# Larger weight-quantisation pieces, a direct attention evacuation, and DMA transposes for three quarters of the gate and up weights

## The reference

```python
scores = einsum(q, k) * 64**-0.5 * exp(-alpha * |i - j|)      # 16 heads of 64
x = layernorm(x + softmax(scores) @ v @ Wo.T + bo)
g = silu(fp4(x) @ fp4(w_gate).T);  u = fp4(x) @ fp4(w_up).T   # w_gate, w_up: 2816 x 1024
x = layernorm(x + fp4(g * u) @ fp4(w_down).T)                 # w_down: 1024 x 2816
```

## Time and profile before

| what | value |
|---|---|
| median of 2 runs | 3286.92 us (3286.06 to 3287.78) |
| the profiled execution, time | 3282.99 us |
| its span, slowest core (core 4) | 3281.4 us |
| spans of the other cores | 3273.2 to 3279.9 us |
| PE busy | 1607.8 us (49%), 7186 instructions |
| DVE busy | 2270.2 us (69%), 3480 instructions |
| ACT busy | 985.7 us (30%), 924 instructions |
| mean granted PE clock | 0.68 of full |

### The profile page before, as it was taken

One profiled execution on the slowest core, in us unless ns is written; L12 is line 12 of the kernel. 1 busy time (PEld: TensorE's weight loads), 2 busy tenths in 40 slices (PEclk: granted clock), 3 DMA queues, 4 the chain that ended last, 5 costly groups with the idle time before them and its releaser, 6 DMA issues.

```text
span 3281.4 us, 26766 instructions; the slowest of 8 cores (3273.2 to 3281.4 us)
## 1 busy us (share of the span) xinstructions
PE 1607.8 (49%) x7186; PEld 548.2 (17%) x7186; DVE 2270.2 (69%) x3480; ACT 985.7 (30%) x924; POOL 36.1 (1%) x61
## 2 busy tenths in 40 slices
PE   5776555555555555555540010000036666663298
PEld 2331111111111111111210000000012222221143
DVE  2006777778777877777358878888868888888223
ACT  1223444444444444444241111111112222222022
POOL 0000000000000000000000000000000000000000
PEclk9886555665566666565775555555568888887599
DMA  5110000000000000000441111111100111111344
GB/s 77 26 26 21 17 19 18 17 19 18 17 19 18 18 19 20 20 20 13 107 153 38 39 52 38 39 39 39 39 13 19 39 38 47 37 39 38 114 172 159
DMA packets 93220, 141.24 MB, mean 43 GB/s; under 512 B 59922, under 2 KB 59922, under 8 KB 93074
## 3 DMA queue, kind: packets, MB, share of 16 engines
q1 hardware_dynamic: 77442, 90.76, 9.0%
q0 software_dynamic: 11024, 31.99, 4.1%
q10 hardware_dynamic: 4608, 16.78, 1.3%
HBM read 104.35 MB, written 36.18 MB: 43 GB/s over the span
## 4 chain that ended last, share of the span: by engine, by line
DVE 53%; PE 19%; issue 14%; ACT 7%; DMA 6%; DVEq 2%; SPq 1%; ACTq 0%; POOL 0%; POOLq 0%
DVE SDr L525 15%; PE ps_o L929 5%; DVE qc L188 4%; DVE qxn L158 4%; DVE qr L151 4%; PE ps_q L328 3%; ACT PT L537 3%; DVE qc L178 2%; DVE qm L183 2%; DVE qc L185 2%; DVE qc L160 2%; PE ps_tp L216 2%; PE ps_av L473 2%; PE ps_q L348 2%; DVE qm L173 2%
## 5 line engine op out<-in xcount | busy, mean ns | idle before, releaser
L525 DVE TENSOR_TENSOR SDr<-ps_s,Wd 128x512 f32<-128x512 f32 x1024 | 637.1, 683 | 251.9 <-PE ps_s L499 218.7
L537 ACT ACTIVATE PT<-SDr 128x2048 bf16<-128x2048 f32 x256 | 474.8, 1902 | 331.2 <-DVE SDr L525 331.2
L499 PE MATMUL ps_s<-QT,KT 64*128 64x512 bf16 x1024 | 280.9, 540 | 453.6 <-DVE SDr L525 452.2
L473 PE MATMUL ps_av<-PT,VV 128*64 128x512 bf16 x1024 | 294.0, 566 | 149.2 <-ACT recD L559 149.2
L164 ACT ACTIVATE qcc<-qc 128x1024 bf16<-128x1024 bf16 (+1 forms) x84 | 99.0, 1179 | 887.8 <-DVE qc L160 887.8
L823 PE MATMUL ps_g<-wgT,x1qT 128*128 128x512 bf16 (+1 forms) x768 | 216.1, 436 | 178.6 <-DVE hbuf L842 178.0
L480 PE MATMUL ps_d<-PT,ones 128*64 128x512 bf16 x1024 | 290.7, 559 | 0.0
L216 PE MATMUL ps_tp<-idn,wqo 128*128 128x128 bf16 x352 | 51.9, 291 | 462.8 <-DVE wqo L189 433.9
L499 PEld LDWEIGHTS ps_s<-QT,KT 64*128 64x128 bf16 x1024 | 59.3, 99 | 815.1 <-issue 815.0
L829 PE MATMUL ps_u<-wuT,x1qT 128*128 128x512 bf16 (+1 forms) x768 | 185.7, 389 | 0.0
L929 PE MATMUL ps_o<-wdT,hin 128*128 128x512 bf16 x704 | 154.8, 384 | 3.2 <-DMA x1in<-x_scr 3.2
(11 more groups left out here) (111 smaller groups left out, 2212.1 us busy)
## 6 DMA issues: line engine op xcount, KB each, us to landing
wst<-wu SPq DMA_DIRECT2D x11, 1024.0 KB
hqT_scr<-hqT POOLq DMA_DIRECT2D x16, 704.0 KB, 3.4
hin<-hqT_scr SPq DMA_DIRECT2D x16, 704.0 KB
awst<-wd SPq DMA_DIRECT2D x16, 512.0 KB
xres<-x SPq DMA_DIRECT2D x16, 512.0 KB, 4.3
x_scr<-ra ACTq DMA_DIRECT2D x16, 512.0 KB, 2.8
x1sl<-x_scr SPq DMA_DIRECT2D x8, 1024.0 KB
x1in<-x_scr SPq DMA_DIRECT2D x16, 512.0 KB
```

The source lines that it names most:

```text
L473: p.do("tensor", lambda e, kt=kt, PT=PT, rq0=rq0, h=h: e.matmul(out=ps_av.ap()[rq0:rq0 + 64, :], lhsT=VVa[:, kt, h * 64:(h + 1) * 64], rhs ...
L499: e.matmul(out=ps.ap()[:, b2 * 512:b2 * 512 + QC], lhsT=KTa[rq0:rq0 + 64, hp, kt * 128:(kt + 1) * 128], rhs=QTa[rq0:rq0 + 64, hp, qc * QC: ...
L525: return e.tensor_tensor(out=SDr.ap()[:, s8 * 512:(s8 + 1) * 512], in0=ps.ap()[:, b2 * 512:b2 * 512 + QC], in1=wd_ap, op=ALU.mult)
L537: e.activation(out=PT.ap()[:, 4 * g * QC:(4 * g + 4) * QC], in_=SDr.ap()[:, r8 * 2048:(r8 + 1) * 2048], func=AF.Exp), sA, 1)
```

## The change

In the attention stage the quantisation scratch is widened from 1024 to 1408 columns, and `w_down` is cut into two pieces of 1408 a row tile, so there are 16 pieces for `w_down` where there were 24, and 24 in all where there were 32; their spacing is 21 steps. `avst` and its copy go: the last multiply of a unit reads `ps_av` in PSUM and waits for `recD`, ACT no longer waits for the earlier multiply, and PE's next accumulation into `ps_av` waits for the multiply (`evac_done`). In the gate and up weights 6 of the 8 column groups of each chunk are transposed by 12 DMAs on SP, and 2 groups remain with PE and DVE.

```diff
--- before.py
+++ after.py
@@ -384,16 +384,15 @@
                 p.wait("tensor", sA, sA_proj)
                 aq_es = ExitStack()
                 aq_sb = lambda n, sh, dt: aq_es.enter_context(nc.sbuf_tensor(n, sh, dt))
-                awst = aq_sb("awst", [128, 1024], F32)
-                awq = aq_sb("awq", [128, 1024], BF16)
-                aqxn = aq_sb("aqxn", [128, 1024], F32)
-                aqc1 = aq_sb("aqc1", [128, 1024], BF16)
-                aqc2 = aq_sb("aqc2", [128, 1024], BF16)
-                aqcc = aq_sb("aqcc", [128, 1024], BF16)
-                aqm = aq_sb("aqm", [128, 1024], I8)
-                aqr = aq_sb("aqr", [128, 64], F32)
-                aqs = aq_sb("aqs", [128, 64], F32)
-                avst = aq_sb("avst", [128, 512], F32)
+                awst = aq_sb("awst", [128, 1408], F32)
+                awq = aq_sb("awq", [128, 1408], BF16)
+                aqxn = aq_sb("aqxn", [128, 1408], F32)
+                aqc1 = aq_sb("aqc1", [128, 1408], BF16)
+                aqc2 = aq_sb("aqc2", [128, 1408], BF16)
+                aqcc = aq_sb("aqcc", [128, 1408], BF16)
+                aqm = aq_sb("aqm", [128, 1408], I8)
+                aqr = aq_sb("aqr", [128, 88], F32)
+                aqs = aq_sb("aqs", [128, 88], F32)
 
                 aqb = {"r": aqr.ap(), "s": aqs.ap(), "xn": aqxn.ap(),
                        "c1": aqc1.ap(), "c2": aqc2.ap(), "cc": aqcc.ap(),
@@ -404,9 +403,10 @@
                 wgq_r2 = wgq_dram.rearrange("(r p) c -> p r c", p=128)
                 aw_chunks = []
                 for rt in range(8):
-                    for (c0, ln) in ((0, 1024), (1024, 768), (1792, 1024)):
-                        aw_chunks.append((wd_r2[:, rt, c0:c0 + ln],
-                                          wdq_r2[:, rt, c0:c0 + ln], ln))
+                    for hf in range(2):
+                        aw_chunks.append((wd_r2[:, rt, hf * 1408:(hf + 1) * 1408],
+                                          wdq_r2[:, rt, hf * 1408:(hf + 1) * 1408],
+                                          1408))
                 for row in range(8):
                     aw_chunks.append((wg_r2[:, row, :], wgq_r2[:, row, :], 1024))
                 aw_load = {}
@@ -453,7 +453,7 @@
 
                 for k in range(len(aw_chunks)):
                     acts = aw_actions(k)
-                    base = k * 16
+                    base = k * 21
                     for oi, off in enumerate((0, 2, 4, 6, 8, 10, 12, 13)):
                         aw_sched[base + off] = acts[oi]
                 wd_stride = 3968
@@ -461,7 +461,6 @@
                 sd_kt = {0: 0, 1: 0, 2: 0}
                 exp_ring = {0: 0, 1: 0}
                 exps_grp = {}
-                evac1_done = {}
                 evac_done = {}
                 recd_done = {}
                 first_sd = True
@@ -507,7 +506,7 @@
                                 up = u - 1
                                 p.wait("tensor", sA, exps_grp[(up, kt // 4)])
                                 if kt == 0:
-                                    p.wait("tensor", sV, evac1_done.get(up - 1, 0))
+                                    p.wait("tensor", sV, evac_done.get(up - 1, 0))
                                     p.wait("tensor", sA, recd_done.get(up - 1, 0))
                                 emit_av_kt(up, kt)
                             p.wait("vector", sT, sT.n)
@@ -548,27 +547,21 @@
                         hp_, qc_ = units[up]
                         if u == len(units):
                             p.wait("tensor", sA, exps_grp[(up, 3)])
-                            p.wait("tensor", sV, evac1_done.get(up - 1, 0))
+                            p.wait("tensor", sV, evac_done.get(up - 1, 0))
                             p.wait("tensor", sA, recd_done.get(up - 1, 0))
                             for kt in range(NTT):
                                 emit_av_kt(up, kt)
                         p.wait("scalar", sT, sT.n)
-                        p.wait("scalar", sV, evac_done.get(up - 1, 0))
                         p.chain("scalar", lambda e: e.activation(
                             out=recD[:, :], in_=ps_d.ap()[:, :], func=AF.Ln), sA)
                         p.chain("scalar", lambda e: e.activation(
                             out=recD[:, :], in_=recD[:, :], func=AF.Exp, scale=-1.0), sA)
                         recd_done[up] = sA.n
+                        p.wait("vector", sA, sA.n)
                         p.wait("vector", sT, sT.n)
-                        p.wait("vector", sV, evac_done.get(up - 1, 0))
-                        p.do("vector", lambda e: e.tensor_copy(
-                            out=avst[:, :], in_=ps_av.ap()[:, :]), sV, 1)
-                        evac1_done[up] = sV.n
-                        p.wait("vector", sV, evac1_done[up])
-                        p.wait("vector", sA, recd_done[up])
                         p.do("vector", lambda e, hp_=hp_, qc_=qc_: e.tensor_tensor(
                             out=QTa[:, hp_, qc_ * QC:(qc_ + 1) * QC],
-                            in0=avst[:, :], in1=recD[:, :], op=ALU.mult), sV, 1)
+                            in0=ps_av.ap()[:, :], in1=recD[:, :], op=ALU.mult), sV, 1)
                         evac_done[up] = sV.n
                 aq_es.close()
             sV_attn = sV.n
@@ -750,6 +743,7 @@
                     ps_tp5 = nc.psum_tensor("ps_tp5", [128, 2048], BF16)
                     ps_tp5t = ps_tp5.__enter__()
                     wqo_reads = [0, 0]
+                    wqo_dmat = [0, 0]
                     wT_done = 0
                     wgq_r = wgq_dram.rearrange("(r p) c -> p r c", p=128)
                     for w_src, wTa, preq, dbgk in ((wg_h, wgTa, 4, "d_wgq"),
@@ -762,10 +756,12 @@
                             wq3 = wqop.rearrange("p (r c) -> p r c", c=D)
                             if ch < preq:
                                 p.wait("sync", sT, wqo_reads[par])
+                                p.wait("sync", tW[par], wqo_dmat[par])
                                 p.wait("sync", dS, dS.n)
                                 p.do("sync", lambda e, ch=ch, wq3=wq3: e.dma_start(
                                     out=wq3, in_=wgq_r[:, 2 * ch:2 * ch + 2, :]), dS, 16)
                                 p.wait("tensor", dS, dS.n)
+                                p.wait("sync", dS, dS.n)
                             else:
                                 p.wait("sync", sV, q_end[par])
                                 p.wait("sync", dS, dS.n)
@@ -775,14 +771,20 @@
                                     in_=w_r[:, 2 * ch:2 * ch + 2, :]), dS, 16)
                                 p.wait("vector", dS, dS.n)
                                 p.wait("vector", sT, wqo_reads[par])
+                                p.wait("vector", tW[par], wqo_dmat[par])
                                 emit_quant(wst.ap()[:, par * I_FF:par * I_FF + 2 * D],
                                            2 * D, qb, wqop)
                                 q_end[par] = sV.n
+                                p.wait("sync", sV, q_end[par])
                                 p.wait("tensor", sV, sV.n)
+                            wqo_dmat[par] = spread_transposes(
+                                [(wTa[:, j, (2 * ch + r2) * 128:(2 * ch + r2 + 1) * 128],
+                                  wq3[:, r2, j * 128:(j + 1) * 128])
+                                 for j in range(6) for r2 in range(2)], tW[par])
                             wqo_reads[par], wT_done = emit_pe_tp(
                                 [(wTa[:, j, 2 * ch * 128:(2 * ch + 2) * 128],
                                   [wq3[:, r2, j * 128:(j + 1) * 128] for r2 in range(2)])
-                                 for j in range(NCT)], ps_tp5t)
+                                 for j in range(6, NCT)], ps_tp5t)
                             if debug and dbgk is not None:
                                 p.wait("gpsimd", sV, sV.n)
                                 p.wait("gpsimd", dS, dS.n)
@@ -801,6 +803,8 @@
                     ic_chunks = [(0, 512), (512, 512), (1024, 512), (1536, 512),
                                  (2048, 512), (2560, 256)]
                     p.wait("tensor", sV, wT_done)
+                    p.wait("tensor", tW[0])
+                    p.wait("tensor", tW[1])
                     sV_sg = {0: sV.n, 1: sV.n}
                     hqTa2 = hqT.ap().rearrange("p (q x) -> p q x", q=2)
                     for tt in range(NTT + 1):
```

## The result

The changed kernel takes 3615.8 us in the median of 11 runs (3592.8 to 3661.8) where the kernel before takes 3287.3 (10 runs): ratio 1.095, 95% interval 1.090 to 1.100. Two of the 11 runs, 3658 and 3662 us, were in a slower state of one half of the chip, and the ratio, of the means, leaves them out. The kernel is slower by about 9.5%; the forecast was 3623 us, in a range of 3575 to 3690. The profiled execution took 3591.5 us, with a span of 3590.0 on its slowest core (core 2), 308.6 more than before.

What follows compares the result with a forecast made beforehand. DVE was taken to set the pace in attention and the gate and up weights. The profiled 3283.0 us, +389 in the weights and -49 in attention, gave 3623 us, 10% slower, range 3575 to 3690.

Steps and rivals of the forecast that it cites:

- evacuation: Attention unit ends: PE waits for the multiply out of PSUM, not only recD; 0.78 us, 31 times, +24 us.
- first four chunks, to the first f32 chunk on DVE: Weight stage start: each loaded-only chunk takes load, wait and twelve transposes, so DVE starts later: +65 us.
- 17 chunk periods: Weight stage: the next load waits behind quantisation and twelve transposes; 45.7 us a chunk against 27.4, +311 us.
- last chunk to the first gate matmul: Weight stage end: PE waits for the last chunk's transposes into tW, 40.5 us against 27.4, +13 us.
- fewer pieces: Attention: wider w_down pieces cut DVE's work by 6.1 us a row tile, 8 times: -49 us.
- actions at step 15: Attention: nine DVE actions fall where DVE waits for recD anyway: -20 us.
- gaps at unit heads: Attention, first steps of a unit: DVE idles 0.26 us a step waiting for PE; changed total -4 us.
- weight stage, and attention: Sums of the forecast: +389 us in the gate and up weights, -49 us in attention.
- Cheap transposes: Rival, weight stage: transposing DMAs take SP no longer than plain loads of their bytes; 3324 us, chance 0.03.
- The slowed load: Rival, weight stage: transposes ahead slow each of 19 loads by 2.33 us; 3668 us, chance 0.07.
- Transposes serialised to their landing: Rival, weight stage: each transpose costs its full landing of 2.33 us; +272, 3896 us, chance 0.03.
- PE in attention: Rival, attention: PE sets the pace, DVE's saving is lost and only +24 remains; 3696 us, chance 0.06.

Runs made afterwards that it cites:

- pieces at 21 steps: Kernel before with only the 1408-column pieces at a spacing of 21 steps, avst and its copy kept: 3217.7 us, ratio 0.979.
- kernel with the waiting load: Kernel before plus one wait: SP loads the next weight chunk only after this chunk's quantisation, no transposing DMAs in that stage: 3305.7 us, ratio 1.0045.
- attention alone: Kernel before with only the change's attention part (wider pieces and direct PSUM read), weight stage as before: 3241.5 us, ratio 0.986.
- kernel with six transposes a chunk: Kernel before with only the weight part, but 3 of 8 column groups by DMA instead of 6: 3499.2 us, ratio 1.061.

## Why the prediction was right

**The mechanism held, but for one wait in the evacuation.** The load begins after the transposes; the two remaining groups are free; the double buffering is lost; the four loaded chunks, the 17 periods and the last chunk each grew.

| term | predicted, us | measured, us |
|---|---|---|
| first four chunks, to the first f32 chunk on DVE | +65 | 82.4 less 22.1 = +60 |
| 17 chunk periods | 45.7 each, +311 | 44.1 each, +285 |
| last chunk to the first gate matmul | +13 | 39.7 less 27.4 = +12 |
| fewer pieces | -49 | -52 |
| actions at step 15 | -20 | -20.7 of DVE's wait |
| gaps at unit heads | -4 | -1 to -3 by core |
| evacuation | +24 | +31 alone, +30 beside the pieces |
| weight stage, and attention | +389, -49 | +357, -46 |

The gaps are read from DVE's waits for PE ahead of SDr in pieces at 21 steps: 30.1 to 32.2 us where there were 33.1. In the mean of eight cores attention is -45.

**The 32 us too much in the weight stage are sizes.** The load was taken from the only exposed one, 6.08 us; in the changed kernel the chunk shown takes 5.4 from issue to DVE's start, where 6.3 was counted. The twelve transposes were read from a group whose second one was held up, 15.9 us; the twelve take 15.3. Together 1.5 us a chunk, 26 us over 17. The smaller ends of both stood among the bounds. The 6.08 was one core's: the same load took 4.83 to 5.10 us on five cores of the same profile of the kernel before, and 6.08 to 6.18 on cores 1, 4 and 6. The first load of the kernel with the waiting load spreads in the same way, 5.0 to 6.3 by core, while the median of the 17 behind it is 4.9 to 5.0 on every core. A term that is counted 18 times should not be taken from one row on one core; x1's 4.96 was the better one.

**The evacuation was mis-sized by a wait that was taken from the wrong pair of engines.** The prediction let PE start 0.13 us after the multiply, as it had started after ACT's `recD`. After a DVE instruction it starts 0.24 us later, and DVE starts 0.16 after `recD`, where 0.09 was kept. That is 0.98 and not 0.78 us a unit. Beside the pieces it is 30 us in the mean of the cores (-44.7 less -74.6). On core 7 it is 27, since that core is among the longest in pieces alone and the shortest in attention alone.

**The rivals.** Cheap transposes are out by the kernel with six transposes a chunk: 1.3 us each. The slowed load is out by every chunk shown: loads were faster than the 6.1 counted. Transposes serialised to their landing are out by twelve in 15.3 us. PE in attention is out by attention alone.

**Some of the closeness is luck.** The forecast of 3623 is 7 us above the median and 32 above the profiled execution, against whose like it was made (3591.5). The growth was forecast at 340 us and is 309 between the two profiles, so it was about a tenth too large; it comes closer to the median because more than half of the 11 runs were 20 us or more longer than the profiled one.

The Trainium skill (Advanced Engine Details and Errata, X-Bar Transpose) had the cheap transposes on its side. The runs do not: twelve tiles of 32 KB in 15.3 us are 26 GB/s, against 350 to 400 expected there. What is paid in the traces is the issue, 1.23 us of SP for every tile; what holds SP for so long, no run here shows.

## What to carry to other kernels

Each transposing DMA occupied the engine that issues it for 1.2 us, and what counted was what stood behind it: before moving work to an idle queue, list what is written after it there and who waits for that. Prefetching by double buffers is only worth the place of the load in program order; put the load first and the slow issuers behind it. Work that has no place on the path can be put where an engine waits for another anyway, if it ends in time.

## What the runs showed of the hardware that I had not expected

- A transposing DMA of 128 x 128 bf16 takes SP 1.20 or 1.23 us in the median, by run, in each of the thirteen kernels: 6, 12 and 16 in a row take 7.3, 15.1 and 19.7 us, the 16 right behind a load (issued at 2017.06, the first transpose at 2017.53). The plain load behind twelve transposes took SP 0.47 us where it takes 0.37 alone.
- At a unit's end PE starts 0.24 us after the DVE instruction that releases it, and it started 0.13 us after the ACT instruction that did before. At 31 hand-overs that is 3 us. The first PE transpose of a chunk, too, starts 0.24 us after DVE (2070.90 to 2071.14).
- The same f32 load of 1024 KB took from 4.82 to 5.80 us in the 18 chunks of the changed kernel's slowest core, and 4.83 to 6.18 over the eight cores of the kernel before, where it is the first of its stage. The cores with about 6.1 are different ones in each profile; why, no run here shows.
